# Retention in a fused two-layer kernel: who opens and who closes its first block

## The chip, the cores and the metric

The kernel runs on one core of a Trainium2 chip. The metric is the device time of one execution in microseconds (us), as the median of several executions. The engines are TensorE (PE in the profile, with PEld for its weight loads), VectorE (DVE), ScalarE (ACT), GpSimd (POOL) and SyncE (SP), which issues most of the DMAs.

## The reference, cut to what matters

Four sublayers run one after the other on `x` (8 batches of 256 rows, 512 columns) with the context `ctx_2048` of the same shape. The change lies in the first of them alone, retention with four heads of 128:

```
xn = layernorm(x)                                # 8 x 256 x 512
Q  = einsum('bshd,hde->bshe', xn,  Wh)
K  = einsum('bshd,hde->bshe', ctx, Wh)
V  = einsum('bshd,hde->bshe', ctx, Wh)
scores = einsum('bshe,bthe->bhst', Q, K) / sqrt(128)
masked = scores * Dn[None]                       # decay mask, never negative
A  = maximum(abs(masked.sum(axis=0)), 1.0)       # one A for all 8 batches
O  = einsum('hst,bthe->bshe', A, V)
Y  = (O - mean) / sqrt(var + 1e-3) * gamma + beta
x  = x + (relu(xn @ wg_w) * Y) @ wo_w
...                                              # bit FFN, mLSTM, mixture of experts
```

The scores are summed over the batches before the absolute value, so nothing of `O` can start until all eight batches have been scored.

## The kernel before, in words

`program` calls `retention`, then `bit_ffn`, `mlstm` and `experts`. `retention` has two blocks. A block is one program for each engine, and all engines meet at its end. Semaphores, set by hand, order the work inside it; each engine runs its own list in the written order.

**First block.** TensorE begins with a setup: it turns `wh` into `ring[0]` (L559, four transposes), clears the three score banks `acc` with products of zeros (L563), and forms `wht`ᵀ`wht` for each head (L566, the "gram"), so that `Q Kᵀ` needs one product with `gram` on the side of `xn` and none on the side of the context. The two results of the setup are copied out of PSUM by VectorE, as `wht` (L509) and `gram` (L511); only then does VectorE take the moments of the first 256 rows (L209 to L216), GpSimd raises the variance to the power -1/2 (L222) and VectorE writes `xn` (L482). TensorE waits for `gram` and for the load of `wg` before its first batch.

Then eight batches run. For one, TensorE turns `xn` and the context (L573, 16 transposes), multiplies `xt` by `gram` (L593, `q`), `ct` by `wh` (L600, `v`), `xt` by `wg` (L610, the gate) and adds the scores into `acc` (L616 into banks 0 and 1 for the first 128 context rows, L618 into bank 2 for the last 128). ScalarE copies `xt` and `qt` and writes the gate through a relu (L536, L540, L544). VectorE copies `ct` and `v` (L488, L505), normalises the next batch and centres the context (L493 to L495). SP stores `ct` and the centred context to `kt_d` and `vc_d`, and reloads `ctx_in` and `x`. Between batches, part of the ternary weights of the FFN is made (L358 on ScalarE, L371 to L383 on VectorE). The first four rounds of ScalarE are a loop, which holds an activation table load at its head.

When all eight batches are scored, VectorE makes `a_t` from `acc` with three instructions over all 1536 columns: times `decay` (L527), maximum of the value and its negative (L528), maximum with 1 (L529). The block ends there.

**Second block.** SP loads `wo`, `gn_gamma`, `gn_beta` and two more FFN weights. TensorE multiplies `a_t` by the values of batch 0 (`pv`, L709 and L712), waits while VectorE normalises the result, turns it (L724), does `pv` of the next batch, and multiplies by `wo` (L736).

Of the kernel before, what the change touches and what calls it, by code (L numbers as in the profile page):

```python
# [15 lines left out]
ALU = mybir.AluOpType  # L16
ACT = mybir.ActivationFunctionType
# [8 lines left out]
P = 128  # L26
B, S, D = 8, 256, 512
# [6 lines left out]
H0 = 4  # L34
# [302 lines left out]
def retention(nc, st, keep, sem, sbuf, psum, a, x, x_rows, ctx_rows, ident, powers, tern, w_mean, raw, vt, turned, kt_d, vc_d, upto):  # L337
    wt = sbuf(st, "gate_t", [P, KD, T])
    at = sbuf(st, "a_t", [P, H0 * (S + P)])
# [51 lines left out]
    with ExitStack() as sa:  # L391
        acc = psum(sa, "acc", [P, 3, 512])
        ring = [psum(sa, f"ring{i}", [P, 512]) for i in range(5)]
        decay = sbuf(sa, "decay", [P, H0 * (S + P)])
        wh = sbuf(sa, "wh", [P, H0, HD])
        wht = sbuf(sa, "wht", [P, H0, HD])
        gram = sbuf(sa, "gram", [P, H0, HD])
# [4 lines left out]
        ct = sbuf(sa, "ct", [P, KD, S])  # L402
        qt = sbuf(sa, "qt", [P, H0, S])
# [5 lines left out]
        ident_in, wh_in, wg_in, decay_in = (sem(n) for n in ("ident_in", "wh_in", "wg_in", "decay_in"))  # L409
        fill_done, dve_step = sem("fill_done"), sem("r_dve_step")  # L410
        setup_ps, setup_sb = sem("setup_ps"), sem("setup_sb")
        xn_ready, xt_ps, ct_ps, xt_sb, ct_sb = (sem(n) for n in ("xn_ready", "xt_ps", "ct_ps", "xt_sb", "ct_sb"))
        q_ps, v_ps, w_ps, q_sb, v_sb, w_sb = (sem(n) for n in ("q_ps", "v_ps", "w_ps", "q_sb", "v_sb", "w_sb"))
        scored, a_ready, kt_out, vc_ready = sem("scored"), sem("a_ready"), sem("kt_out"), sem("vc_ready")
        vc_out = [sem(f"vc_out{u}") for u in range(2)]
        block = sa.enter_context(nc.Block())
# [55 lines left out]
        @block.vector  # L472
        def _(dve):
            steps = Steps(dve, dve_step)

            def normalise(b, i, u):
                dve.wait_ge(x_in[u], 16 * i + 16)
                norm.stats(steps, [x[:, CB * b + c, :] if isinstance(b, int) else x[:, ds(CB * b + c, 1), :]
                                   for c in range(CB)], LN_EPS)
                dve.wait_ge(norm.rstd_ready, b + 1)  # L480
                for c in range(CB):
                    nc.vector.tensor_scalar(xn[:, c, :], x[:, ds(CB * b + c, 1), :], norm.mv[:, c, 0:1],  # L482
                                            norm.rstd[:, c:c + 1], ALU.subtract, ALU.mult).then_inc(xn_ready, 1)

            def copies(b, src_sem, counts, ring_at, dst, done):
                for c in range(CB):
                    dve.wait_ge(src_sem, 2 * b + c + 1)
                    nc.vector.tensor_copy(dst(c), ring[ring_at[c]][:].rearrange("p (k n) -> p k n", n=P)).then_inc(done, 1)  # L488

            def centre(u):  # L490

                heads = cx[:, u].rearrange("p c (h e) -> p c h e", e=DH)
                steps.then(nc.vector.tensor_reduce(vmean[:], heads, AX.X, ALU.add))  # L493
                steps.then(nc.vector.tensor_scalar(vmean[:], vmean[:], 1.0 / DH, None, ALU.mult))
                nc.vector.tensor_tensor(heads, heads, vmean[:].unsqueeze(3).to_broadcast([P, CB, NH, DH]),  # L495
                                        ALU.subtract).then_inc(vc_ready, 1)

            def batch(b, u, nxt):
                dve.wait_ge(kt_out, 16 * b + 16)
                copies(b, ct_ps, None, (1, 3), lambda c: ct[:, :, c * P:(c + 1) * P], ct_sb)  # L500
                if nxt is not None:
                    normalise(b + 1, *nxt)
                for c in range(CB):
                    dve.wait_ge(v_ps, 2 * b + c + 1)
                    nc.vector.tensor_copy(vt[:, ds(CB * b + c, 1), :], ring[1 + c][:]).then_inc(v_sb, 1)  # L505
                centre(u)

            dve.wait_ge(setup_ps, 1)
            nc.vector.tensor_copy(wht[:], ring[0][:].rearrange("p (h n) -> p h n", n=P)).then_inc(setup_sb, 1)  # L509
            dve.wait_ge(setup_ps, 2)  # L510
            nc.vector.tensor_copy(gram[:], ring[1][:].rearrange("p (h n) -> p h n", n=P)).then_inc(setup_sb, 1)  # L511
            normalise(0, 0, 0)
            dve.sem_inc(kt_out, 16)
            with steps.loop(0, B // 2 - 1, 12) as i:
                batch(2 * i, 0, (i, 1))
                batch(2 * i + 1, 1, (i + 1, 0))
            half = KF * D // 2
            dve.wait_ge(mean_ready, 1)
            ternary(steps, [(0, raw)], 0, half)
            batch(B - 2, 0, (B // 2 - 1, 1))  # L520
            ternary(steps, [(0, raw)], half, half)
            batch(B - 1, 1, None)

            dve.wait_ge(scored, B)
            dve.wait_ge(decay_in, 16)
            flat = acc[:].rearrange("p n d -> p (n d)")
            steps.then(nc.vector.tensor_tensor(at[:], flat, decay[:], ALU.mult))  # L527
            steps.then(nc.vector.scalar_tensor_tensor(at[:], at[:], -1.0, at[:], ALU.mult, ALU.max))  # L528
            nc.vector.tensor_scalar(at[:], at[:], 1.0, None, ALU.max).then_inc(a_ready, 1)  # L529

        @block.scalar
        def _(act):
            def batch(b):
                for c in range(CB):
                    act.wait_ge(xt_ps, 2 * b + c + 1)
                    nc.scalar.copy(xt[:, :, c * P:(c + 1) * P],  # L536
                                   ring[2 * c][:].rearrange("p (k n) -> p k n", n=P)).then_inc(xt_sb, 1)
                for c in range(CB):
                    act.wait_ge(q_ps, 2 * b + c + 1)
                    nc.scalar.copy(qt[:, :, c * P:(c + 1) * P],  # L540
                                   ring[(4, 0)[c]][:].rearrange("p (k n) -> p k n", n=P)).then_inc(q_sb, 1)
                for c in range(2):
                    act.wait_ge(w_ps, 2 * b + c + 1)
                    nc.scalar.activation(wt[:, 2 * c:2 * c + 2, ds(S * b, S)],  # L544
                                         ring[3 + c][:].rearrange("p (k n) -> p k n", n=S), ACT.Relu).then_inc(w_sb, 1)

            with act.Fori(0, B - 4) as b:
                batch(b)
            abs_sum(act, 0, raw)
            with act.Fori(B - 4, B) as b:  # L550
                batch(b)

        @block.tensor
        def _(pe):
# [3 lines left out]
            for h in range(H0):  # L558
                last = nc.tensor.transpose(ring[0][:, h * P:(h + 1) * P], wh[:, h, :], ident[:])  # L559
# [3 lines left out]
                nc.tensor.matmul(acc[:, n, :], zeros[:, 0:P], zeros[:], start=True, stop=False, skip_group_check=True)  # L563
            pe.wait_ge(setup_sb, 1)
            for h in range(H0):
                last = nc.tensor.matmul(ring[1][:, h * P:(h + 1) * P], wht[:, h, :], wht[:, h, :], start=True, stop=True)  # L566
            last.then_inc(setup_ps, 1)
            pe.wait_ge(setup_sb, 2)
            pe.wait_ge(wg_in, 16)

            def turn(dst, src, done):
                for k in range(KD):
# [3 lines left out]
            def batch(b, i, u, first=False):  # L576
                for c in range(CB):
# [7 lines left out]
                        pe.wait_ge(*((v_sb, 2 * b - 1), (w_sb, 2 * b - 1))[c])  # L585
                    turn(ring[2 * c + 1], cx[:, u, c, :], ct_ps)

                for c in range(CB):
                    pe.wait_ge(xt_sb, 2 * b + c + 1)
                    if c == 0 and not first:  # L590
                        pe.wait_ge(w_sb, 2 * b)
                    for h in range(H0):
                        last = nc.tensor.matmul(ring[(4, 0)[c]][:, h * P:(h + 1) * P], gram[:, h, :],  # L593
                                                xt[:, h, c * P:(c + 1) * P], start=True, stop=True)
                    last.then_inc(q_ps, 1)

                for c in range(CB):
# [3 lines left out]
                                                wh[:, h, :], start=True, stop=True)  # L601
                    last.then_inc(v_ps, 1)

                for n in range(2):
                    if n == 1:
                        pe.wait_ge(q_sb, 2 * b + 1)
                    for j in range(2):
                        m = 2 * n + j
                        for k in range(KD):
                            last = nc.tensor.matmul(ring[3 + n][:, j * S:(j + 1) * S], wg[:, k, m * P:(m + 1) * P],  # L610
                                                    xt[:, k, :], start=k == 0, stop=k == KD - 1)
                    last.then_inc(w_ps, 1)

                pe.wait_ge(q_sb, 2 * b + 2)
                for h in range(H0):
                    nc.tensor.matmul(acc[:, h // 2, (h % 2) * S:(h % 2 + 1) * S], ct[:, h, 0:P], qt[:, h, :],  # L616
                                     start=False, stop=False, skip_group_check=True)
                    last = nc.tensor.matmul(acc[:, 2, h * P:(h + 1) * P], ct[:, h, P:S], qt[:, h, P:S],  # L618
                                            start=False, stop=False, skip_group_check=True)
                last.then_inc(scored, 1)  # L620
# [2229 lines left out]
```

## Time and profile before

| | us |
|---|---|
| three executions | 1164.37, 1163.9, 1161.15 |
| median | 1163.9 |
| the profiled execution | 1158.16 |
| its span, from the first instruction to the last | 1156.4 |
| outside the span (1158.16 - 1156.4) | 1.76 |
| first block of retention, first to last instruction | 0 to 142.84 |

All times in the rows below are microseconds from the start of the span. TensorE is busy for 1075.6 of the 1156.4 us, VectorE for 839.1, ScalarE for 476.2 and GpSimd for 440.5. The granted clock is a share of TensorE's upper level of 2.4 GHz: 1.00 is that level, 0.50 is 1.2 GHz. Its mean over the span is 0.965.

### The profile page before, as it was taken

The numbers are of one execution on the slowest core, as the hardware profiler recorded it, in microseconds if no ns is written. First come the engines' busy times: TensorE is split into PE (matmuls) and PEld (weight loads), VectorE is DVE, ScalarE is ACT, GpSimd is POOL, SyncE is SP. The second block draws the span as 40 slices with busy tenths as digits, with TensorE's granted clock in tenths as the row PEclk, the third lists the DMA queues.
The fourth block names the chain that finished last, engine by engine and source line by source line (L and its number), as shares of the span: only waits on it lengthen the run. The fifth ranks groups of instructions, "written<-read, shape, count | busy, mean of one in ns | idle before, by whom it ended". The sixth has DMA issues, their size and how long they took to land. (4 is left out here: it accounts for less than half of the span.)

```text
span 1156.4 us, 21710 instructions
## 1 busy us (share of the span) xinstructions
PE 1075.6 (93%) x5911; PEld 814.0 (70%) x5912; DVE 839.1 (73%) x1578; ACT 476.2 (41%) x1009; POOL 440.5 (38%) x355
## 2 busy tenths in 40 slices
PE   6999889989998799999899987999999999999997
PEld 5989765634443458988887765777777777777773
DVE  4537545969998648778897994868688687766656
ACT  1342125336564269888521162333333333333320
POOL 0001011315442100667662001556665556666620
PEclk8999999999999898989889997999999999999998
DMA  7344162243233587755075313889899899887759
GB/s 275 128 146 154 56 244 41 46 83 69 56 68 60 156 266 261 254 191 183 1 266 201 65 56 126 238 191 246 190 259 264 202 261 252 196 200 189 138 120 367
DMA packets 148189, 195.49 MB, mean 169 GB/s; under 512 B 62985, under 2 KB 80777, under 8 KB 148144
## 3 DMA queue, kind: packets, MB, share of 16 engines
q1 hardware_dynamic: 130512, 156.61, 42.7%
q0 software_dynamic: 17632, 38.32, 16.7%
q8 instruction: 23, 0.38, 0.1%
q14 instruction: 22, 0.18, 0.0%
HBM read 136.56 MB, written 50.34 MB: 162 GB/s over the span
## 5 line engine op out<-in xcount | busy, mean ns | idle before, releaser
L2442 POOL DMA_INDIRECT y_d<-tail,x_ox x78 | 142.8, 1830 | 126.4 <-ACT tail L2669 105.8
L1718 POOL DMA_INDIRECT e_rows<-r_d,x_ix x80 | 101.6, 1270 | 115.5 <-issue 95.9
L2514 PE MATMUL x_h<-x_w_hi,x_t_hi 128*128 x320 | 127.8, 399 | 2.2 <-DVE x_t_lo L2683 2.2
L2515 PE MATMUL x_h<-x_w_lo,x_t_hi 128*128 x320 | 127.6, 399 | 0.0
L2516 PE MATMUL x_h<-x_w_hi,x_t_lo 128*128 x320 | 127.5, 399 | 0.0
L2683 DVE TENSOR_TENSOR x_w_lo<-w,x_w_hi (+1 forms) x64 | 112.5, 1759 | 9.8 <-ACT x_w_hi L2640 2.6
L2631 ACT ACTIVATE e_rows<-x_h 128x256 f32<-128x256 f32 x80 | 30.8, 385 | 183.7 <-PE x_h L2516 183.6
L222 POOL TENSOR_TENSOR ln_rstd<-ln_ve,powers 128x2 f32<-128x2 f32 (+1 forms) x40 | 34.5, 861 | 174.0 <-DVE ln_ve L216 174.0
L2683 DVE TENSOR_TENSOR x_t_lo<-x_xb,x_t_hi 128x512 fp32r<-128x512 f32 x80 | 55.2, 691 | 45.4 <-ACT x_t_hi L2626 43.7
L2533 PE MATMUL x_o<-x_w_hi,x_avt_hi 128*128 x160 | 74.0, 462 | 1.0 <-issue 0.7
L1595 DVE SCALAR_TENSOR_TENSOR raw<-h_qk,h_d 128x768 f32<-128x768 f32 x64 | 58.2, 952 | 22.1 <-ACT h_d L1362 10.1
L2514 PEld LDWEIGHTS x_h<-x_w_hi,x_t_hi 128*128 128x128 f32 x320 | 60.8, 190 | 17.5 <-issue 2.6
L2515 PEld LDWEIGHTS x_h<-x_w_lo,x_t_hi 128*128 128x128 f32 x320 | 60.8, 190 | 14.8
L2516 PEld LDWEIGHTS x_h<-x_w_hi,x_t_lo 128*128 128x128 f32 x320 | 60.7, 190 | 14.8
L1361 ACT ACTIVATE h_d<-h_negm,h_g 128x256 f32<-128x256 f32 x128 | 63.6, 497 | 6.2 <-DVE h_negm L1575 3.0
L736 PE MATMUL p_bank<-wo,z_t 128*128 128x512 f32 x128 | 58.3, 610 | 6.9 <-DVE z_t L799 6.9
L2730 DVE SCALAR_TENSOR_TENSOR e_rows<-e_rows,x_rw,x_h 128x256 f32<-128x256 f32 x80 | 38.2, 478 | 35.1 <-ACT e_rows L2631 34.4
L2534 PE MATMUL x_o<-x_w_lo,x_avt_hi 128*128 x160 | 63.3, 395 | 0.0
L610 PE MATMUL ring<-xt,wg 128*128 128x256 f32 x256 | 56.6, 379 | 0.0
L1488 PE MATMUL h_pv<-h_v,raw 128*128 128x99 f32 x256 | 55.3, 300 | 0.0
L2669 ACT COPY tail<-x_o 128x512 f32<-128x512 f32 x78 | 45.9, 589 | 18.6 <-PE x_o L2539 18.6
L1489 PE MATMUL h_pv<-h_v,raw 128*128 128x99 f32 x256 | 52.7, 290 | 0.0
(420 smaller groups left out, 2584.4 us busy)
## 6 DMA issues: line engine op xcount, KB each, us to landing
w<-in_L_ffn_w SPq DMA_DIRECT2D x32, 1024.0 KB, 9.5
w<-in_L_ffn_w SPq DMA_DIRECT2D x32, 512.0 KB, 8.5
h_negm<-negm_d SPq DMA_DIRECT2D x15, 1024.0 KB, 7.6
raw<-in_L_ffn_w SPq DMA_DIRECT2D x3, 2816.0 KB, 16.5
x_res<-in_x SPq DMA_DIRECT2D x8, 512.0 KB, 4.6
ctx_in<-in_ctx SPq DMA_DIRECT2D x8, 512.0 KB, 3.5
kt_d<-ct SPq DMA_DIRECT2D x8, 512.0 KB, 3.2
vc_d<-ctx_in SPq DMA_DIRECT2D x8, 512.0 KB, 2.6
```

What stands on the lines that cost most here:

```text
L610: last = nc.tensor.matmul(ring[3 + n][:, j * S:(j + 1) * S], wg[:, k, m * P:(m + 1) * P], xt[:, k, :], start=k == 0, stop=k == KD - 1)
L736: last = nc.tensor.matmul(p_bank[c][:], zt[:, c, k * P:(k + 1) * P], wo[:, k, :], start=k == 0, stop=k == KD - 1)
L1361: nc.scalar.activation(dm[:, k % 2, j, 0:2, :], nm[:, u, h, 0:2, :], ACT.Exp, bias=gst[:, u, 0, h:h + 1])
L1595: nc.vector.scalar_tensor_tensor(cm[:, k % 2, heads], qk[:, heads, 0:3 * P], float(DH) ** -0.5, dm[:, k % 2, heads].rearrange("p j c n -> ...
L1718: nc.gpsimd.indirect_dma_start(out=xg[q][s], out_offset=None, in_=r_d, in_offset=bass.IndirectOffsetOnAxis(ap=ix[q][:, s:s + 1], axis=0), ...
L2442: nc.gpsimd.indirect_dma_start(out=y_d[s], out_offset=bass.IndirectOffsetOnAxis(ap=ox[q][:, s:s + 1], axis=0), in_=eo[q][s][:], in_offset= ...
L2514: nc.tensor.matmul(hbank[s], hi[:, k, :], w13p[0][:, at, k, :], start=k == 0, stop=False)
L2515: nc.tensor.matmul(hbank[s], hi[:, k, :], w13p[1][:, at, k, :], start=False, stop=False)
L2516: last = nc.tensor.matmul(hbank[s], lo[:, k, :], w13p[0][:, at, k, :], start=False, stop=k == KD - 1)
L2533: nc.tensor.matmul(obank[s], hi[:, f, :], w2p[0][:, at, f, :], start=f == 0, stop=False)
L2534: nc.tensor.matmul(obank[s], hi[:, f, :], w2p[1][:, at, f, :], start=False, stop=False)
L2683: return nc.vector.tensor_tensor(dst, src, hi.bitcast(F32), ALU.subtract)
```

## The change

- VectorE no longer copies `wht` and `gram`. Its list begins with the moments of the first rows. ScalarE makes both copies, ahead of its loop over the batches, and the gram is formed in `ring[4]` instead of `ring[1]`.
- TensorE no longer waits for `gram` and `wg` ahead of its first transposes, but ahead of the first product that reads each.
- In every batch the four products L616 come before the four L618, and the semaphore `scored` counts each bank by itself.
- `a_t` is formed bank by bank. ScalarE writes the absolute value of a bank of `acc` to `a_t`; VectorE multiplies it by `decay` in place and takes the maximum with 1. The decay mask is never negative, so the absolute value may come first.

```diff
             def batch(b, u, nxt): ...
-            dve.wait_ge(setup_ps, 1)
-            nc.vector.tensor_copy(wht[:], ring[0][:].rearrange("p (h n) -> p h n", n=P)).then_inc(setup_sb, 1)
-            dve.wait_ge(setup_ps, 2)
-            nc.vector.tensor_copy(gram[:], ring[1][:].rearrange("p (h n) -> p h n", n=P)).then_inc(setup_sb, 1)
             normalise(0, 0, 0)
...
-            dve.wait_ge(scored, B)
             dve.wait_ge(decay_in, 16)
-            flat = acc[:].rearrange("p n d -> p (n d)")
-            steps.then(nc.vector.tensor_tensor(at[:], flat, decay[:], ALU.mult))
-            steps.then(nc.vector.scalar_tensor_tensor(at[:], at[:], -1.0, at[:], ALU.mult, ALU.max))
-            nc.vector.tensor_scalar(at[:], at[:], 1.0, None, ALU.max).then_inc(a_ready, 1)
+            def decayed(n):
+                dve.wait_ge(abs_scores, n + 1)
+                mine = slice(n * D, (n + 1) * D)
+                return nc.vector.tensor_tensor(at[:, mine], at[:, mine], decay[:, mine], ALU.mult)
+            def floored(n):
+                mine = at[:, n * D:(n + 1) * D]
+                nc.vector.tensor_scalar(mine, mine, 1.0, None, ALU.max).then_inc(a_ready, 1)
+            steps.then(decayed(0))
+            floored(0)
+            steps.did(decayed(1))
+            steps.then(decayed(2))
+            floored(1)
+            floored(2)
...
+            act.wait_ge(setup_ps, 1)
+            nc.scalar.copy(wht[:], ring[0][:].rearrange("p (h n) -> p h n", n=P)).then_inc(setup_sb, 1)
+            act.wait_ge(setup_ps, 2)
+            nc.scalar.copy(gram[:], ring[4][:].rearrange("p (h n) -> p h n", n=P)).then_inc(setup_sb, 1)
             with act.Fori(0, B - 4) as b:
...
+            for n in range(3):
+                act.wait_ge(scored, 3 * B - 2 + n)
+                nc.scalar.activation(at[:, n * D:(n + 1) * D], acc[:, n, :], ACT.Abs).then_inc(abs_scores, 1)
...
-                last = nc.tensor.matmul(ring[1][:, h * P:(h + 1) * P], wht[:, h, :], wht[:, h, :], start=True, stop=True)
+                last = nc.tensor.matmul(ring[4][:, h * P:(h + 1) * P], wht[:, h, :], wht[:, h, :], start=True, stop=True)
             last.then_inc(setup_ps, 1)
-            pe.wait_ge(setup_sb, 2)
-            pe.wait_ge(wg_in, 16)
```

TensorE's list at the very start, before: the first product of a batch (`ring<-ident,xn`) stands behind three waits, `setup_sb` among them.

```order
L559 MATMUL ring<-ident,wh 128x128 [waits fill_done,wh_in,ident_in]
L559 MATMUL ring<-ident,wh 128x128 x3
L563 MATMUL acc<-zeros 128x512 x3
L566 MATMUL ring<-wht 128x128 [waits setup_sb]
L566 MATMUL ring<-wht 128x128 x3
L573 MATMUL ring<-ident,xn 128x128 [waits xn_ready,wg_in,setup_sb]
L573 MATMUL ring<-ident,xn 128x128 x3
L573 MATMUL ring<-ident,ctx_in 128x128 [waits ctx_in0]
```

The same place now, up to the gate's first product (`ring<-xt,wg`):

```order
L574 MATMUL ring<-ident,wh 128x128 [waits fill_done,wh_in,ident_in]
L574 MATMUL ring<-ident,wh 128x128 x3
L578 MATMUL acc<-zeros 128x512 x3
L581 MATMUL ring<-wht 128x128 [waits setup_sb]
L581 MATMUL ring<-wht 128x128 x3
L586 MATMUL ring<-ident,xn 128x128 [waits xn_ready]
L586 MATMUL ring<-ident,xn 128x128 x3
...
L608 MATMUL ring<-xt,gram 128x128 [waits xt_sb,setup_sb]
...
L627 MATMUL ring<-xt,wg 128x256 [waits wg_in]
```

The wait for `gram` moved behind the 16 transposes, and the wait for `wg` behind the products `q` and `v` too.

VectorE's list at the end of the first block, before, from the last batch's copies of `v` on:

```order
L505 COPY v_rows<-ring 128x512 [waits v_ps] x2
L493 TENSOR_REDUCE v_mean<-ctx_in 128x32
L494 TENSOR_SCALAR v_mean<-v_mean 128x32 [waits r_dve_step]
L495 TENSOR_TENSOR ctx_in<-ctx_in,v_mean 128x1024 [waits r_dve_step]
L527 TENSOR_TENSOR a_t<-acc,decay 128x1536 [waits decay_in,scored]
L528 SCALAR_TENSOR_TENSOR a_t<-a_t 128x1536 [waits r_dve_step]
L529 TENSOR_SCALAR a_t<-a_t 128x1536 [waits r_dve_step]
```

The same place now; ahead of it, as the last instruction of its own list in this block, ScalarE has `L566 ACTIVATE a_t<-acc 128x512 [waits scored] x3`, a line number of the changed file.

```order
L506 COPY v_rows<-ring 128x512 [waits v_ps] x2
L494 TENSOR_REDUCE v_mean<-ctx_in 128x32
L495 TENSOR_SCALAR v_mean<-v_mean 128x32 [waits r_dve_step]
L496 TENSOR_TENSOR ctx_in<-ctx_in,v_mean 128x1024 [waits r_dve_step]
L526 TENSOR_TENSOR a_t<-a_t,decay 128x512 [waits abs_scores,decay_in]
L530 TENSOR_SCALAR a_t<-a_t 128x512 [waits r_dve_step]
L526 TENSOR_TENSOR a_t<-a_t,decay 128x512 [waits abs_scores] x2
L530 TENSOR_SCALAR a_t<-a_t 128x512 [waits r_dve_step]
L530 TENSOR_SCALAR a_t<-a_t 128x512
```

Three instructions over 1536 columns became three products and three maxima over 512 columns, and the absolute value went to ScalarE.

## Rows read from the trace of the kernel before

**Rows 1.** The page: TensorE over the whole span, then its granted clock in tenths.

```profile
PE 1075.6 (93%) x5911; PEld 814.0 (70%) x5912; DVE 839.1 (73%) x1578; ACT 476.2 (41%) x1009; POOL 440.5 (38%) x355
PEclk8999999999999898989889997999999999999998
```

**Rows 2.** Timeline, first 15 us: start, duration, engine, line, operation, count, [idle before <-releaser].

```profile
8.34 1.92 PE L566 MATMUL ring<-wht 128*128 128x128 f32 x8
10.29 0.69 DVE L511 COPY gram<-ring 128x512 f32<-128x512 f32 x1 [2.30 <-PE ring L566]
10.90 1.28 DVE L209 BATCH_NORM_STATS2 ln_st<-x_res 128x6 f32<-128x512 f32 x2
14.34 1.09 PE L573 MATMUL ring<-ident,xn 128*128 128x128 f32 x4 [4.08 <-DVE xn L482]
```

**Rows 3.** DMA issues at 0.7, 2.2, 2.75, 18 us; last number is us to landing.

```profile
x_res<-in_x SPq DMA_DIRECT2D x1, 512.0 KB, 3.5
...
ctx_in<-in_ctx SPq DMA_DIRECT2D x1, 512.0 KB, 6.2
...
wg<-in_L_xattn_wg_w SPq DMA_DIRECT2D x1, 1024.0 KB, 8.4
...
kt_d<-ct SPq DMA_DIRECT2D x1, 512.0 KB, 5.0
```

**Rows 4.** Windows: stretch, length, busy of PE, PEld, DVE, ACT, POOL, clock, DMA, GB/s.

```profile
10.30:13.60 3.30, 0.00 (x0) 0.00 (x0) 2.35 (x7) 0.00 (x0) 0.72 (x1) 1.00 1.05 389
14.30:17.80 3.50, 3.46 (x17) 3.49 (x18) 1.04 (x2) 1.17 (x2) 0.00 (x0) 0.50 1.05 388
17.80:20.40 2.60, 2.60 (x14) 2.60 (x14) 2.31 (x7) 0.59 (x1) 0.00 (x0) 0.50 1.04 387
```

**Rows 5.** Timeline of TensorE: batch 0's `v` and gate, then batch 7's transposes and `v`.

```profile
20.82 1.95 PE L600 MATMUL ring<-wh,ct 128*128 128x128 f32 x16
22.61 7.07 PE L610 MATMUL ring<-xt,wg 128*128 128x256 f32 x32
...
123.25 0.60 PE L573 MATMUL ring<-ident,xn 128*128 128x128 f32 x4
...
126.78 1.95 PE L600 MATMUL ring<-wh,ct 128*128 128x128 f32 x16
```

**Rows 6.** Waits from 30 to 138 us, TensorE's only one: total, times, longest.

```profile
PE ring L593 <- ACT xt L536: 1.8, 1, 1.8
```

**Rows 7.** Timeline at the end of the first block and the start of the second.

```profile
135.76 0.60 ACT L544 ACTIVATE gate_t<-ring 128x512 f32 x1 [2.86 <-PE ring L610]
137.87 0.38 PE L618 MATMUL acc<-qt,ct 128*128 128x128 f32 x2
138.29 1.76 DVE L527 TENSOR_TENSOR a_t<-acc,decay 128x1536 f32<-128x1536 f32 x1 [6.23 <-PE acc L618]
141.88 0.96 DVE L529 TENSOR_SCALAR a_t<-a_t 128x1536 f32<-128x1536 f32 x1
143.17 0.66 PE L709 MATMUL o_bank<-v_rows,a_t 128*128 128x128 f32 x2 [4.92 <-PEq L391]
```

**Rows 8.** Groups of instructions, 0 to 160 us: busy, mean ns of one, idle before.

```profile
L377 DVE TENSOR_SCALAR raw<-raw 128x2816 f32<-128x2816 f32 x2 | 3.3, 1628 | 0.1
L799 DVE TENSOR_TENSOR z_t<-z_t,gate_t 128x512 f32<-128x512 f32 x2 | 1.4, 691 | 2.4 <-ACT z_t L756 2.4
```

**Rows 9.** Windows of the second block; columns as in rows 4.

```profile
143.40:146.70 3.30, 3.30 (x17) 3.30 (x17) 0.00 (x0) 0.00 (x0) 0.00 (x0) 0.50 0.62 189
153.60:156.90 3.30, 3.30 (x18) 3.30 (x17) 1.38 (x2) 2.35 (x7) 0.00 (x0) 0.50 1.06 400
183.30:185.80 2.50, 0.00 (x0) 0.00 (x0) 2.36 (x9) 1.67 (x2) 0.55 (x1) 1.00 0.51 101
185.80:193.00 7.20, 7.18 (x18) 3.31 (x19) 4.38 (x11) 7.20 (x3) 1.50 (x4) 1.00 0.00 0
```

**Rows 10.** Issue of `gn_beta` at 144.1 us, with its time to landing.

```profile
gn_beta<-in_L_xattn_gn_beta SPq DMA_DIRECT2D x1, 2.0 KB, 5.1
```

**Rows 11.** Timeline of ScalarE between batches 0 and 1.

```profile
30.42 1.28 ACT L536 ACT_TABLE_LOAD   x1
32.77 0.59 ACT L536 COPY xt<-ring 128x512 f32<-128x512 f32 x1 [1.06 <-PE ring L573]
```

**Rows 12.** Windows: first and last of ten later stretches at the lower clock.

```profile
242.30:245.70 3.40, 3.40 (x5) 1.34 (x5) 1.86 (x2) 1.02 (x2) 0.00 (x0) 0.50 0.09 19
...
710.00:720.10 10.10, 6.05 (x18) 4.82 (x19) 5.96 (x6) 4.33 (x7) 0.00 (x0) 0.50 0.39 141
```

More of the change, by code:

```diff
@@ L413, in retention @@
         q_ps, v_ps, w_ps, q_sb, v_sb, w_sb = (sem(n) for n in ("q_ps", "v_ps", "w_ps", "q_sb", "v_sb", "w_sb"))
+        abs_scores = sem("abs_scores")
         scored, a_ready, kt_out, vc_ready = sem("scored"), sem("a_ready"), sem("kt_out"), sem("vc_ready")
@@ L586, in batch @@
                     turn(ring[2 * c + 1], cx[:, u, c, :], ct_ps)
+                if first:
+                    pe.wait_ge(setup_sb, 2)
                 for c in range(CB):
@@ L602, in batch @@
                     last.then_inc(v_ps, 1)
+                if first:
+                    pe.wait_ge(wg_in, 16)
                 for n in range(2):
@@ L615, in batch @@
                 for h in range(H0):
-                    nc.tensor.matmul(acc[:, h // 2, (h % 2) * S:(h % 2 + 1) * S], ct[:, h, 0:P], qt[:, h, :],
-                                     start=False, stop=False, skip_group_check=True)
+                    last = nc.tensor.matmul(acc[:, h // 2, (h % 2) * S:(h % 2 + 1) * S], ct[:, h, 0:P], qt[:, h, :],
+                                            start=False, stop=False, skip_group_check=True)
+                    if h % 2:
+                        last.then_inc(scored, 1)
+                for h in range(H0):
                     last = nc.tensor.matmul(acc[:, 2, h * P:(h + 1) * P], ct[:, h, P:S], qt[:, h, P:S],
```

## The prediction

> **What bounds the kernel.** I read the page first, then the timeline of the first 30 us, then the timeline and the waits around the block's end at 138 us, and last the granted clock of the same stretches. TensorE is busy for 93% of the span [rows 1], and inside the eight batches it waits once, for 1.8 us, between 30 and 138 us [rows 6]. So the first block is a chain of TensorE work with a hole at each end, and what shortens a hole moves everything after it. The reader is to see the two holes. TensorE ends the gram at 8.34 + 1.92 = 10.26 and starts its first transposes at 14.34, after 4.08 us in which VectorE copies `gram` and only then opens the moments [rows 2]. It ends the scores at 137.87 + 0.38 = 138.25 and starts on `a_t` at 143.17, 4.92 us later, while VectorE runs three long instructions [rows 7]. A third thing is seen in the clock: the work that follows each hole runs at the lower level, 1.2 GHz (0.50), from 14.3 to 20.4 and from 143.4 to 146.7 [rows 4, 9].
>
> **Head, the hole.** From VectorE's first moment to TensorE's first transpose the chain takes 14.34 - 10.90 = 3.44 us [rows 2]. The rows that it needs are issued at the start of the program and take 3.5 us to land [rows 3]; the issue lies between 0.7 and 1.2 us, so they are there by 4.7 at the latest. `xn` is then ready at about 4.7 + 3.4 = 8.1, ahead of 10.26. TensorE's setup itself stays as long: ScalarE's copy of `wht` takes about as long as its 0.59 us copy of `xt` [rows 11], against 0.69 for a VectorE copy of 512 columns [rows 2], and it is hidden by the clearing products. The transposes can start at 10.26: **4.08 us are gone**. What is late next? The context is issued by 2.7 and takes 6.2, so it lands by 8.9; `wg` is issued by 3.2 and takes 8.4, so by 11.6, and its first reader now comes after the transposes, `q` and `v`, not before 15 [rows 3]. The gram copy on ScalarE (0.6 us, to about 10.9) stands ahead of the first copy of `xt` in ScalarE's queue; that copy can't start before TensorE has turned four blocks (0.6 to 1.1 us, by the level of the clock [rows 2, 5], from 10.26), so at most 0.2 us is added there, and TensorE has the other transposes to do meanwhile. Nothing else is queued behind the two copies. The store of `ct` now comes some 6 us earlier, under the load of the FFN weights; before it was issued at 18.9 and took 5.0 us [rows 3]. VectorE waits for it only ahead of batch 1's `ct`, more than 8 us after the issue in either kernel; I count nothing.
>
> **Head, the clock.** The trace grants 1.00 from 10.3 to 13.6, where TensorE has nothing to do, just after the matmuls of the setup. It grants 0.50 from 14.3 on, through the transposes and until 20.4, when 2.6 us of matmuls have run [rows 4]. From the first transpose to the start of `v` takes 20.82 - 14.34 = 6.48 us in batch 0 and 126.78 - 123.25 = 3.53 us in batch 7 at the upper level [rows 5]. So that stretch costs 2.95 us for the level alone. With the hole closed the batch falls into the stretch that is granted 1.00, directly behind 3 us of setup matmuls, and in the steady batches a block of 16 transposes between matmuls keeps 1.00. I take the whole **2.95 us**. The bounds are 0 (the clock stays low for as much work as before) and 2.95.
>
> **Table loads.** ScalarE's loop carried a table load of 1.28 us in each of its rounds; now one stands ahead of the loop. ScalarE was idle for 1.06 us behind the load, waiting for TensorE [rows 11]. That wait is the cover, and the gain is nothing. The one load left has 5 us before `wht` is asked for.
>
> **Inside the batches.** The scores are the same eight products in another order, with two more increments. No engine waits for them before the last batch. Nothing, within 0.1 us a batch.
>
> **Tail, the hole.** The last product still ends at 138.25, in this trace's times. Bank 0 is complete about 1.8 us ahead, bank 1 about 0.9 us ahead. ScalarE ends the gate's relu at 136.36 [rows 7] and is free for bank 0. The absolute value of a bank has no row of its own; the relu of 512 columns from PSUM takes 0.60 [rows 7], and that is what I take (0.59 for a copy, rows 11, is the other end). Bank 2: 138.3 + 0.60 = 138.9. VectorE's product of 512 columns in SBUF takes 0.69 [rows 8]; banks 0 and 1 are done by 138.95, bank 2 runs to 139.65. The maximum with 1 is 0.96 for 1536 columns and 1.63 for 2816 [rows 7, 8], so 0.67 / 1280 a column, and 0.96 - 1024 x 0.00052 = 0.42 for 512; by a share of a third it would be 0.32. Two of them end at 139.7 + 0.42 + 0.35 = 140.45. Before, the chain ended at 141.88 + 0.96 = 142.84. **The gain is 2.4 us** (2.2 to 2.6 with the bounds of the two unseen durations), and the meeting of the engines behind it, 143.17 - 142.84 = 0.33, stays. What the three whole instructions cost and the pieces don't is hidden under TensorE's last products.
>
> The trace has 0.69 for a product of 512 columns where a third of 1.76 would be 0.59 [rows 7, 8], so each piece pays a fixed part. The Trainium skill, "VectorE: DVE Perf Modes", section "Rules for kernel authors", says that chained VectorE operations should be cut in number, which speaks against six in place of three. Taken alone it would make the tail three fixed parts longer, three times about 0.15 us by these rows, and the sum smaller by that 0.45 us; the rows show why it does not decide, since four of the six lie beside other work.
>
> **Tail, the clock.** `pv` of batch 0 runs at 0.50 from 143.4 to 146.7 [rows 9]. At the upper level these 3.3 us of work are 1.65. The hole ahead of it shrinks from 4.92 to 2.5 us. The nearest row is a hole of 2.5 us from 183.3 to 185.8, after which the clock stays at 1.00 [rows 9]. Against it: after the next hole of 3.7 us, which stays, the clock falls again at 153.6. The bounds are 0 and 1.65; which executions keep the clock will differ, and I count the middle, **0.8 us**. Nothing else holds this back: `gn_beta`, issued by 144.4, lands by 149.5, and moves with the block [rows 10]; TensorE's next transposes came 9.1 us after the block's start, and would come at 7.5, when it has landed at 6.3.
>
> **Sum.** 4.08 + 2.95 + 2.4 + 0.8 = 10.2 us. Against the profiled execution's own 1158.16 that is 1147.9. That execution was 5.7 us below the median of the runs shown, 1163.9; all of its holes are before the same semaphores, so I take the difference from the median: **1153.7 us**.
>
> **Rivals.**
> - *The clock stays low through the head (20%).* From 14.3 to 17.8 TensorE did transposes only, at 0.50, and the level rose only after matmuls [rows 4]. If the 16 transposes behind the gram drop or hold it, batch 0 runs as slowly as before and only the hole is gained: 4.08 + 2.4 + 0 to 1.65 = 6.5 to 8.1, about 1156.6. For it: 3.5 us of transposes did not raise the clock. Against it: in batch 7 the same transposes ran at full pace [rows 5]. The Trainium skill, "TensorE: Matmul & The Clock Gate", section "Part 4: PE-mode transpose", says that transposes don't count as activity in the way matmuls do; by that rule this rival would hold. Batch 0's rows agree with it, and batch 7's do not refute it, since matmuls stand close on both sides there.
> - *The clock stays up in both places (25% of the forecast's 70%).* 4.08 + 2.95 + 2.4 + 1.65 = 11.1, so 1152.8.
> - *The head does not open early (5%).* If VectorE or GpSimd starts late, because `xn` hangs on something that the trace of before did not show (its first moments at 10.90 were behind a copy, so no earlier start was ever seen), only the tail is left: 2.4 to 4.1, so 1160 to 1161.5, within what a measurement tells from no change. The same holds if the change does not do what it says.
> - *Slower (3%).* Behind 160 us there are ten stretches at 0.50, 60 us together, the first of 3.4 us and the last of 10.1 [rows 12], each after an idle spell of TensorE in the later layers. The change moves the later program against the clock's grants by 10 us. A stretch of 3.4 us costs at most 1.7. To end over 0.3% slower, it must lose 10.2 + 3.5 = 13.7 us, eight more such stretches, which gives 1168. The executions of before, which differ in just this way, spread over 6.2 us from 1158.16 to 1164.37, so half of that price is not seen.
>
> **How the numbers follow.** The forecast (one or the other tail clock, full head) has 70%, with 1151 to 1155.5 as its own span; the low-clock head 20%; the late head 5%; slower 3%; a gain above 13 us 2%. The executions differ by some 3 us about their median, and 0.3% of 1163.9 is 3.5 us, about what a measurement of this kernel can tell from no change. The range runs from 1163.9 - 11.1 - 3 = 1149.8 to 1163.9 - 6.5 + 2.5 = 1159.9. Faster by over 0.3% (below 1160.4) 0.90, within it 0.07, slower 0.03.
>
> **What would show it right or wrong.** In the profile after: the first moments near 4.5 us; the first `xn` transposes with no idle before them, at 10.3; the granted clock at 1.00 until past 20; the gate products of batch 0 starting near 15.6 and not 22.6. At the end of the block: ScalarE's third absolute value 0.6 us long, the last maximum 2.2 us behind TensorE's last score, and `pv` 2.5 us behind it, at about 0.1 us a product if the clock held, and not at 0.2 (17 products in 3.3 us, rows 9). Between the two, the batches at an unchanged pitch. It is wrong if TensorE waits for `gram`, `ct` or `wg` in batch 0, if the batches lose what the head gains, or if the later layers give it back.

## The result

| | before | changed |
|---|---|---|
| median of four executions, us | 1163.05 | 1150.22 |
| lowest and highest | 1161.15 to 1164.37 | 1146.71 to 1151.06 |
| profiled execution | 1158.16 | 1151.06 |
| its span | 1156.4 | 1149.2 |

The ratio is 0.9898, with a 95% interval from 0.9871 to 0.9925: 12 us less, 8.7 to 15.0. Timed again, six executions of the changed kernel had a median of 1149.42 against 1160.57 for seventeen of before, a ratio of 0.9898 once more (0.9876 to 0.9920), 11.8 us less. What was expected of this second timing was 9.4 to 11.1 us less, with a rival of 12 us or more that would mean something beyond the two ends of the block; its interval, from 9.3 to 14.4 us, holds both. The forecast was 1153.7 in a range from 1149.8 to 1159.9, a gain of 10.2 us. The measured median lies near the low end of that range, and 0.8 us below the 1151 to 1155.5 that the forecast gave as its own span.

### The profile page after: what moved, and what is told of

Read it like the earlier page. It is cut to its first block and busy times, and to the rows that moved or that the text cites. A ratio compares the mean times of both kernels' runs of the same rounds, so it can differ in the third digit from the quotient of the medians.

```text
span 1149.2 us, 21701 instructions
## 1 busy us (share of the span) xinstructions
PE 1072.1 (93%) x5899; PEld 813.8 (71%) x5912; DVE 836.3 (73%) x1579; ACT 475.3 (41%) x1011; POOL 444.5 (39%) x355
## 5 line engine op out<-in xcount | busy, mean ns | idle before, releaser
L2534 PEld LDWEIGHTS x_h<-x_w_hi,x_t_hi 128*128 128x128 f32 x320 | 60.9, 190 | 17.5 <-issue 2.6
```

What stands on the lines that cost most here:

```text
L2534: nc.tensor.matmul(hbank[s], hi[:, k, :], w13p[0][:, at, k, :], start=k == 0, stop=False)
```

## The profile after

TensorE's share of the span is the same 93% as in [rows 1]; what it waits for has changed. The timeline of TensorE at the start, to be held against [rows 2] (line numbers are those of the changed file: L586 was L573, L581 was L566):

```profile
8.70 1.76 PE L581 MATMUL ring<-wht 128*128 128x128 f32 x8
10.30 0.60 PE L586 MATMUL ring<-ident,xn 128*128 128x128 f32 x4
```

No idle time stands at the first transposes, they start at 10.30 and not at 14.34, and four of them take 0.60 us and not 1.09. What feeds them, from the same timeline:

```profile
4.28 1.28 DVE L209 BATCH_NORM_STATS2 ln_st<-x_res 128x6 f32<-128x512 f32 x2 [4.13 <-DMA x_res<-in_x]
7.03 1.00 DVE L483 TENSOR_SCALAR xn<-x_res,ln_mv,ln_rstd 128x512 f32<-128x512 f32 x2 [0.92 <-POOL ln_rstd L222]
10.50 0.59 ACT L558 COPY gram<-ring 128x512 f32<-128x512 f32 x1 [2.24 <-PE ring L581]
13.83 1.95 PE L615 MATMUL ring<-wh,ct 128*128 128x128 f32 x16
15.62 7.07 PE L627 MATMUL ring<-xt,wg 128*128 128x256 f32 x32
```

VectorE waits for the first rows, and `xn` is there two microseconds before TensorE wants it. The gate's products of batch 0 start at 15.62, against 22.61 in [rows 5]: 7.0 us ahead. In the batches that follow TensorE waits once, for the same 1.8 us as in [rows 6].

The end of the block, against [rows 7] (L638 was L618, L729 was L709):

```profile
129.55 0.60 ACT L566 ACTIVATE a_t<-acc 128x512 f32<-128x512 f32 x1 [0.18 <-PE acc L633]
130.21 1.05 PE L638 MATMUL acc<-qt,ct 128*128 128x128 f32 x8
130.25 0.69 DVE L526 TENSOR_TENSOR a_t<-a_t,decay 128x512 f32<-128x512 f32 x1 [5.18 <-ACT a_t L566]
131.30 0.60 ACT L566 ACTIVATE a_t<-acc 128x512 f32<-128x512 f32 x1 [0.29 <-PE acc L638]
131.32 1.31 DVE L526 TENSOR_TENSOR a_t<-a_t,decay 128x512 f32<-128x512 f32 x2
132.66 0.76 DVE L530 TENSOR_SCALAR a_t<-a_t 128x512 f32<-128x512 f32 x2
133.75 0.46 PE L729 MATMUL o_bank<-v_rows,a_t 128*128 128x128 f32 x2 [2.49 <-PEq L391]
```

The last score ends at 131.26 and VectorE's last maximum at 133.42, 2.16 us later. TensorE's hole is 2.49 us and was 4.92. `pv` starts 9.42 us ahead of before.

The granted clock, from the windows of the changed kernel (stretch, length, busy of PE, PEld, DVE, ACT, POOL, clock, DMA, GB/s), against [rows 4, 9]:

```profile
10.30:13.90 3.60, 3.60 (x35) 3.60 (x34) 2.35 (x4) 2.25 (x4) 0.00 (x0) 1.00 1.03 380
13.90:20.40 6.50, 6.50 (x40) 5.93 (x40) 5.44 (x12) 1.18 (x2) 0.71 (x1) 1.00 1.05 390
133.80:137.50 3.70, 3.70 (x32) 3.57 (x32) 0.00 (x0) 0.00 (x0) 0.05 (x2) 1.00 0.61 217
141.30:146.40 5.10, 5.10 (x24) 5.10 (x25) 1.93 (x3) 2.90 (x8) 0.00 (x0) 0.50 1.05 394
```

Batch 0 runs at the upper level all through, and so does `pv` of batch 0. The low stretch behind the next hole, 3.4 us long in the trace of before, is 6.8 us long here, from 139.9 to 146.7. That length is not the change's doing: in a second profile of the kernel before, the same stretch is 6.8 us long too, from 151.7 to 158.5.

**Where the time went, stage by stage.** The table gives, for each profiled execution, the start of the last product with `wo` (the end of the second block, within a microsecond) and what is left from there to the end of the span. The rows below the first four are the experiments of the next section.

| execution | last product with `wo` | from there to the end |
|---|---|---|
| before | 250.3 | 906.1 |
| before, again | 251.6 | 906.7 |
| changed | 240.0 | 909.2 |
| changed, again | 239.2 | 908.7 |
| head alone | 242.9 | 908.2 |
| tail alone | 246.7 | 911.9 |
| tail alone, again | 247.7 | 910.0 |
| before, head filled | 248.1 | 912.3 |
| before, tail filled | 249.5 | 908.2 |
| changed, both holes filled | 237.9 | 910.8 |
| changed, second hole filled | 238.8 | 909.1 |
| changed, gram first | 239.4 | 908.2 |
| changed, more transposes | 246.4 | 905.3 |
| changed, more products | 246.6 | 909.8 |

The first column holds the change: 250.3 and 251.6 before, 240.0 and 239.2 after, 11.4 us between the means. The second column belongs to layers that no edit touches, and it runs from 905.3 to 912.3 in no order that the edits explain: the two profiles of the changed kernel lie about 2.5 us above the two of before, but the two kernels that are before with a hole filled, which share nothing with the change, lie 1.8 and 5.9 us above them. Single executions therefore differ by several microseconds, and the two profiled executions of the head of this section, 7.1 us apart, understate the change.

## Experiments

Each was timed against the kernel before on the same chip. As a scale, the kernel before was timed against itself:

> The kernel before, timed against itself. Both theories: a ratio of 1 within 0.25%, which says how far the other ratios can be trusted. Its profile should show the hole of 4.1 us at the head with the clock at 0.50 behind it, the hole of 4.9 us at the tail, and the last product with wo near 250; from there to the end of the span 905 to 913 us, as in the other executions, whatever was done in the first block.

Measured: ratio 0.9996 (0.9973 to 1.0020), medians 1161.09 and 1161.89. So differences under about 2.5 us are not shown by times alone, and the profiles have to tell them.

**The head alone.** The copies of `wht` and `gram` on ScalarE, VectorE opening with the moments, the two waits of TensorE moved; the scores and `a_t` as before.

```diff
-            dve.wait_ge(setup_ps, 1)
-            nc.vector.tensor_copy(wht[:], ...).then_inc(setup_sb, 1)
-            dve.wait_ge(setup_ps, 2)
-            nc.vector.tensor_copy(gram[:], ...).then_inc(setup_sb, 1)
...
+            act.wait_ge(setup_ps, 1)
+            nc.scalar.copy(wht[:], ...).then_inc(setup_sb, 1)
+            act.wait_ge(setup_ps, 2)
+            nc.scalar.copy(gram[:], ...).then_inc(setup_sb, 1)
```

> Only the head of the change: VectorE opens with the moments, ScalarE copies wht and gram, TensorE's waits for gram and wg moved; scores and a_t as before. Theory: 4.1 for the hole and 2.95 for the clock, so 7.0 us less than before, pv starting near 136.2, and the clock at 0.50 in pv of batch 0 as before. Rival that the clock is no part of it: 4.1 us.

Measured: ratio 0.9941 (0.9917 to 0.9964), 6.8 us less (4.2 to 9.6). Its `pv` starts at 135.77, 7.4 us ahead of the first profile of before and 6.4 us ahead of the second, behind the old hole and at the old pace:

```profile
135.77 0.47 PE L711 MATMUL o_bank<-v_rows,a_t 128*128 128x128 f32 x2 [4.92 <-PEq L391]
135.70:139.10 3.40, 3.33 (x17) 3.36 (x18) 0.00 (x0) 0.00 (x0) 0.13 (x2) 0.56 0.58 191
```

The first line is from its timeline, the second from its windows. The 4.1 us of the rival are just outside the interval, and the profile rules them out: from the first transpose to `v` it takes 3.54 us, where before takes 6.48.

**The tail alone**, timed twice: the scores by bank, ScalarE's absolute value and VectorE's pieces; the head as before.

```diff
+            for n in range(3):
+                act.wait_ge(scored, 3 * B - 2 + n)
+                nc.scalar.activation(at[:, n * D:(n + 1) * D], acc[:, n, :], ACT.Abs).then_inc(abs_scores, 1)
```

> Only the tail of the change: scores counted by bank, ScalarE's absolute value, VectorE bank by bank; the head as before. Theory: 2.4 us for the hole, 0 to 1.65 for the clock in pv of batch 0, so 2.4 to 4.1 less than before. Batch 0 has the hole of 4.1 us and the low clock as before. Rival that the two ends don't add up (the tail's gain hangs on the head): less than 2 us.

Measured: ratio 0.9944 (0.9921 to 0.9966), 6.5 us less (3.9 to 9.2). That was more than the theory allows for, and I timed it once more.

> The tail of the change alone once more. Theory: 2.4 to 4.1 us less than before; the 6.5 us of its first timing, with an interval from 3.9 to 9.2, were the spread of the later layers. Rival (the tail is worth more than its hole and one low stretch): again 5 us or more.

Measured: ratio 0.9973 (0.9948 to 0.9998), 3.1 us less (0.2 to 6.0), and in the table its second block ends 4.3 and, in the second profile, 3.3 us ahead of the mean of before. The rival's 5 us or more lie inside the interval, but the table speaks against them: what the first timing had on top was the spread. The second profile also holds something that the changed kernel's does not: here the hole of 2.5 us did cost the clock. The products L727 and L730 of its `pv` go from 0.39 us a pair to 0.63:

```profile
139.61 0.46 PE L727 MATMUL o_bank<-v_rows,a_t 128*128 128x128 f32 x2 [2.49 <-PEq L391]
139.91 0.39 PE L730 MATMUL o_bank<-v_rows,ones 128*128 128x128 f32 x2
140.13 0.39 PE L727 MATMUL o_bank<-v_rows,a_t 128*128 128x128 f32 x2
140.35 0.56 PE L730 MATMUL o_bank<-v_rows,ones 128*128 128x128 f32 x2
140.71 0.63 PE L727 MATMUL o_bank<-v_rows,a_t 128*128 128x128 f32 x2
```

**The head's hole kept, but filled.** The kernel before, with 15 products of zeros by zeros between the gram and the wait for it. They add nothing to the cleared bank.

```diff
             last.then_inc(setup_ps, 1)
+            for _ in range(15):
+                nc.tensor.matmul(acc[:, 0, :], zeros[:, 0:P], zeros[:], start=False, stop=False, skip_group_check=True)
             pe.wait_ge(setup_sb, 2)
```

> The kernel before, with 15 products of zeros by zeros (added onto the cleared score bank, which they leave as it is) in TensorE's hole between the gram and the first transposes. The hole stays as long, about 4.1 us, but TensorE is at work in it. Clock theory: the granted clock is 1.00 from 10 to 24 us, the first transpose stays at about 14.3, v of batch 0 starts 3.5 us behind it and not 6.5, and the kernel is 2.95 us faster. Rival (the clock of batch 0 is set by the transposes and not by the hole): 0.50 from 14 to 20 as before, no gain.

Measured: ratio 0.9980 (0.9959 to 1.0002), 2.3 us less (from 4.8 less to 0.2 more). The times alone would not show it; the profile does. Its timeline and its windows:

```profile
9.58 4.26 PE L569 MATMUL acc<-zeros 128*128 128x512 bf16 x15
13.87 0.63 PE L575 MATMUL ring<-ident,xn 128*128 128x128 f32 x4
17.43 1.84 PE L602 MATMUL ring<-wh,ct 128*128 128x128 f32 x15
14.30:17.80 3.50, 3.50 (x34) 3.50 (x33) 2.62 (x5) 1.93 (x4) 0.00 (x0) 1.00 1.04 387
```

From the first transpose to `v` are 17.43 - 13.87 = 3.56 us, where before had 6.48 [rows 5], at a clock of 1.00 where before had 0.50 [rows 4]. The hole is as long as it was (from 9.79 to 13.87). So of the head's 7 us, 2.9 are the clock, and they come from TensorE having been at work just before, not from anything in batch 0. The filling did more than keep a level: its 15 products take 4.26 us, 0.28 each, where the same product takes 0.22 in a profile further down (24 in 5.34 us). The first of them still ran at the lower pace, and the level came up while they ran.

**The tail's hole kept, but filled.** The kernel before, with 20 products of zeros behind the last batch.

```diff
                 batch(2 * i + 1, i, 1)
+            for _ in range(20):
+                nc.tensor.matmul(ring[0][:], zeros[:, 0:P], zeros[:], start=True, stop=True)
```

> The kernel before, with 20 products of zeros in TensorE's hole of 4.9 us ahead of pv; the hole stays as long. Clock theory: pv of batch 0 runs at 1.00 and ends 1.65 us sooner behind its start, so 1.65 us less than before. Rival (the gain of 6.5 us that the tail alone showed, against 2.4 to 4.1 expected, is the clock and is worth more than one low stretch): 3 us or more less than before.

Measured: ratio 0.9979 (0.9961 to 0.9997), 2.4 us less (0.3 to 4.5). `pv` of batch 0, in its windows, against the first line of [rows 9]:

```profile
142.80:146.40 3.60, 3.58 (x32) 3.60 (x32) 0.00 (x0) 0.00 (x0) 0.11 (x2) 1.00 0.66 184
```

Thirty-two products where before had 17 in 3.3 us. The rival's 3 us or more lie inside the interval, but the table has 1.5 us, and with the second timing of the tail nothing is left to explain.

**The changed kernel, its holes filled.** In one kernel 9 products of zeros in the hole of 2.5 us and 14 of ones by ones in the hole of 3.7 us behind `pv`; in the other the second set alone.

```diff
                 batch(2 * i + 1, i, 1)
+            for _ in range(9):
+                nc.tensor.matmul(ring[0][:], zeros[:, 0:P], zeros[:], start=True, stop=True)
...
             pv(0)
+            for _ in range(14):
+                nc.tensor.matmul(p_bank[0][:, 0:P], ones[:], ones[:], start=True, stop=True)
             pe.wait_ge(wo_in, 48)
```

> The changed kernel with 9 products of zeros (into a bank nobody reads any more) in TensorE's hole of 2.5 us at the end of the first block and 14 small products of ones by ones in its hole of 3.7 us behind pv of batch 0; both sets fit into their holes. Clock theory: nothing starts later, the low stretch from 139.6 to 146.4 of the changed kernel is gone, its 5.1 us of work take half, so 2.5 us less than the changed kernel, 12 to 14 us less than before. Rival (the low stretch there does not come from the hole, or only moves on): as the changed kernel.

> As after_filled_both, with only the hole of 3.7 us behind pv of batch 0 filled. If the hole of 2.5 us ahead of pv never costs the clock, this gains the same 2.5 us over the changed kernel; if it sometimes does, this gains less than after_filled_both by up to 1.65 us.

Measured: ratios 0.9895 (0.9876 to 0.9913) and 0.9885 (0.9864 to 0.9906), medians 1149.64 and 1147.34. The windows of the kernel with both, for the second hole and for what follows it:

```profile
137.60:141.50 3.90, 3.36 (x31) 3.17 (x29) 2.69 (x8) 0.00 (x0) 0.69 (x1) 1.00 0.89 277
141.50:146.20 4.70, 4.66 (x40) 4.45 (x41) 2.00 (x3) 2.90 (x8) 0.00 (x0) 1.00 1.05 395
```

The low stretch is gone, 40 products run where the changed kernel had 24, and the first product with `wo` comes 12.2 us behind `pv`'s start and not 14.6. The second block ends 1.7 us ahead of the mean of the changed kernel. In the whole time this can't be told from the changed kernel. In the kernel with the second hole filled alone a low stretch turned up from 173.5 to 176.8 us, where neither profile of the changed kernel has one, so in that execution a part of it may have moved on. Neither is shown to be faster than the change itself.

The kernel with both holes filled shows one thing more. Its head is that of the changed kernel, closed, and yet batch 0 begins at the lower pace:

```profile
9.82 1.06 PE L586 MATMUL ring<-ident,xn 128*128 128x128 f32 x4
10.67 0.93 PE L586 MATMUL ring<-ident,ctx_in 128*128 128x128 f32 x4
11.44 0.60 PE L586 MATMUL ring<-ident,xn 128*128 128x128 f32 x4
```

From the first transpose to `v` it takes 14.10 - 9.82 = 4.28 us, 0.75 more than the changed kernel. So a closed head does not always save the whole of the clock's price.

**The wait for gram back ahead of the transposes**, in the changed kernel.

```diff
             last.then_inc(setup_ps, 1)
+            pe.wait_ge(setup_sb, 2)
...
-                if first:
-                    pe.wait_ge(setup_sb, 2)
```

> The changed kernel, with TensorE's wait for gram put back ahead of its first transposes. Theory: TensorE stands from 10.3 until ScalarE has copied gram, about 11.1, so 0.8 us more than the changed kernel, with the clock at 1.00 all through batch 0. Rival (most of the head's gain comes from the moved wait): 4 us or more.

Measured: ratio 0.9904 (0.9878 to 0.9929), 11.1 us less than before. The timeline has the price of the wait, 0.68 us, with the transposes at full pace behind it:

```profile
10.35 0.66 PE L587 MATMUL ring<-ident,xn 128*128 128x128 f32 x4 [0.68 <-ACT gram L558]
10.84 0.60 PE L587 MATMUL ring<-ident,ctx_in 128*128 128x128 f32 x4
```

So the head's hole was closed by VectorE opening with the moments; moving the wait is worth the last 0.7 us of it. What moving the wait for `wg` is worth was not tried. In the changed kernel that load is issued at 2.8 to 3.3 and takes 8.2 us, so it lands at 11.0 to 11.5, behind the first transposes at 10.30: by these rows up to about 1 us may hang on it, an estimate.

**Do transposes hold the clock?** Two variants of the changed kernel with more work ahead of batch 0: 48 transposes of rows that are turned anyway, or 24 products of zeros.

```diff
+            pe.wait_ge(xn_ready, 1)
+            for _ in range(12):
+                for k in range(KD):
+                    nc.tensor.transpose(ring[2][:, k * P:(k + 1) * P], xn[:, 0, k * P:(k + 1) * P], ident[:])
             batch(0, 0, 0, first=True)
```

> The changed kernel with 48 more transposes of the same rows ahead of batch 0, some 5.3 us at the upper level. If transposes hold the clock as matmuls do, it stays at 1.00 and batch 0 starts 5.3 us later. If they don't, the clock falls to 0.50 in or right behind them, the last of them are twice as far apart, and part of batch 0 runs at half pace: 7 to 9 us later than the changed kernel.

> The partner of after_more_turns: 24 products of zeros by zeros in place of the 48 transposes, some 5.2 us at the upper level. Both theories: the clock stays at 1.00 and batch 0 starts 5.2 us later than in the changed kernel.

Measured: 1153.45 and 1158.19, one execution each, so nothing rests on these times. The timeline and the windows of the kernel with more transposes, and last the 24 products of its partner:

```profile
9.55 5.58 PE L645 MATMUL ring<-ident,xn 128*128 128x128 f32 x48
14.96 0.60 PE L586 MATMUL ring<-ident,xn 128*128 128x128 f32 x4
16.71 1.95 PE L608 MATMUL ring<-xt,gram 128*128 128x128 f32 x16
9.60:15.00 5.40, 5.40 (x50) 5.40 (x49) 0.00 (x0) 0.59 (x1) 0.00 (x0) 1.00 1.05 395
15.00:16.70 1.70, 1.70 (x18) 1.70 (x16) 0.66 (x1) 0.81 (x2) 0.00 (x0) 1.00 1.05 389
10.13 5.34 PE L644 MATMUL ring<-zeros 128*128 128x512 bf16 x24
```

For 7.1 us, from 9.55 to 16.71, TensorE did nothing but transposes, and the last of them still run at the upper pace, 0.60 us for four, as they do behind the products. That is one execution, of float32 transposes that began about when the level came up.

Whether transposes can also bring a low clock up is seen in the second profile of the tail alone, whose head is that of before. Its timeline, then its windows:

```profile
14.79 1.09 PE L588 MATMUL ring<-ident,xn 128*128 128x128 f32 x4 [4.08 <-DVE xn L483]
17.38 0.69 PE L588 MATMUL ring<-ident,ctx_in 128*128 128x128 f32 x4
17.90 1.95 PE L608 MATMUL ring<-xt,gram 128*128 128x128 f32 x16
14.80:17.50 2.70, 2.70 (x13) 2.70 (x14) 0.99 (x2) 0.59 (x1) 0.00 (x0) 0.50 1.05 388
17.60:17.90 0.30, 0.30 (x4) 0.30 (x4) 0.00 (x0) 0.28 (x1) 0.00 (x0) 1.00 1.08 403
```

The clock fell to 0.50 at 14.1, inside the hole. From 14.79 on TensorE did only transposes, and at 17.5, before the first product with `gram` at 17.90, it was back at 1.00. So they can, in this one execution; in the other four with the open hole it came back among the products of `q`.

## Why the prediction was right

**The head's hole, 4.08 us: right.** The first transposes moved from 14.34 to 10.30, and the cover named for every later input held: `xn` by 8.0, `gram` copied by 11.1, nothing waited for in batch 0. **The head's clock, 2.95 us: the mechanism right and its cause shown, the size taken at its largest.** From the first transpose to `v` the changed kernel takes 13.83 - 10.30 = 3.53 us, against 6.48. The filled hole gives the same 2.9 with the hole kept. Of the profiled executions, all five with the open hole had a low stretch in batch 0 (one of them by its pace alone, see the last section). It took them 6.48, 5.66, 6.34, 4.90 and 6.37 us from the first transpose to `v`, so the price was between 1.4 and 2.95 us, 2.4 in the mean. Of the nine with the hole closed or filled, eight took 3.5 to 3.6 us, and one took 4.28 (the changed kernel with both later holes filled). The whole of the head was 7.0 us in the first pair of profiles, as forecast, and 6.8 in the second (21.64 - 14.80 at the gate's first product).

**The rival of the transposes fell.** It had 20%, and rested on transposes that ran at 0.50 without raising the clock. The extra transposes show that they hold a level that is already there, and the second profile of the tail alone that they can run a low one up. The Trainium skill, "TensorE: Matmul & The Clock Gate", section "Part 4: PE-mode transpose", says that transposes don't count as activity in the way matmuls do; here the run of 64, still at the upper pace at its end, and the rise at 17.5 in the midst of transposes speak against it for this case, and the measurement decides.

**The tail's hole, 2.4 us: right.** 4.92 - 2.49 = 2.43, with the pieces as costed: 597 ns for the absolute value, 690 for a product and 424 for a maximum of 512 columns, in the grouped rows of the changed kernel:

```profile
L526 DVE TENSOR_TENSOR a_t<-a_t,decay 128x512 f32<-128x512 f32 x3 | 2.0, 690 | 5.2 <-ACT a_t L566 5.2
L566 ACT ACTIVATE a_t<-acc 128x512 f32<-128x512 f32 x3 | 1.8, 597 | 0.7 <-PE acc L633 0.4 <-PE acc L638 0.3
L530 DVE TENSOR_SCALAR a_t<-a_t 128x512 f32<-128x512 f32 x3 | 1.2, 424 | 0.1
```

One point of it was only touched on, where banks 0 and 1 are done by 138.95 and the last absolute value by 138.9: VectorE works without a pause from 130.25 to 133.42, so the last bank does not set the end alone. Bank 0's absolute value, at 129.55, starts a chain on VectorE of six pieces that is as long.

**The tail's clock, 0.8 us as the middle of 0 and 1.65: the right mechanism, but the upper bound was too low.** In both profiled executions of the changed kernel the whole price was saved: from `pv`'s start to VectorE's first look at its result are 3.85 us, where the first profile of before had 5.47. The bound of 1.65 came from that one trace, in which the clock falls at 143.3, just behind `pv`'s start. In the second profile of before it falls at 141.5, inside the hole, and stays low until 148.3:

```profile
142.30:148.00 5.70, 5.70 (x27) 5.70 (x28) 0.00 (x0) 0.00 (x0) 0.00 (x0) 0.50 0.75 207
```

There the same stretch takes 148.93 - 142.20 = 6.73 us. Over the four executions with the hole of 4.9 us the price was 1.6, 2.9, 1.6 and 2.2 us. Of the eight profiled executions with a hole of 2.5 us, five kept the clock in `pv` of batch 0 and three lost it (the second of the tail alone and the two with more work ahead); all four with the hole of 4.9 us lost it, and neither of the two with it filled did.

**What the sum left out.** By VectorE's first look at `pv` the changed kernel was 148.64 - 137.60 = 11.04 us ahead in the profiled pair, and by the first product with `wo` 158.64 - 148.34 = 10.30: the clock fell once more behind the next hole, for 6.8 us against 3.4 in this pair. I had named that hole and left its cost unchanged, and the second profile of before, with 6.8 us there too, does not contradict that. Over the two blocks the gain is 11.4 us in the means of two executions each, and 10.2 was forecast. The terms, in the same means and up to VectorE's first look at `pv` (11.6 us): the head's hole, with the setup ahead of it, 4.4 where the sum had 4.08; the head's clock 2.5 where it had 2.95; the tail's hole 2.4 as forecast; the tail's clock 2.25 where it had 0.8. The tail's clock is the term that was mis-sized, and part of it is hidden by the head's clock, which was counted too high.

**The step down to the median** was right in sign. I took the sum off the median of before and not off the profiled execution, 5.7 us lower. The table gives half of a reason: that execution's later layers took 906.1 us, against 908.9 in the mean of the fourteen, 2.8 us of the 5.7. The measured gain of 12 us, with its interval from 8.7 to 15.0, holds both 10.2 and 11.4, and the times alone don't say whether the whole is more than the two blocks show. The slower rival had the same mechanism, later stretches at the lower clock, and it is real, as spread: the second column of the table spans 7.0 us. It didn't move with the change.

## What to carry to other kernels

A hole in TensorE's work costs its own length and then again, because the work behind it can run at half pace; here the second price was 1.4 to 2.9 us for a hole of 4.1 (five executions) and 1.6 to 2.9 for one of 4.9 (four). One trace is not enough to size it: in the two profiles of the kernel before, the clock fell at different places of the same hole and stayed low for 3.4 us in one and 6.8 us in the other. Look at who makes the first operand of a stage, and let that engine open with it; copies that the same engine does on the side go to one that is idle. Where a chain of elementwise steps stands behind the last product, cut it by bank, so that little more than the last bank's share is left when TensorE stops (2.2 us here, where the whole chain took 4.6).

## What the runs showed that I had not expected

- A hole of 2.5 us is on the edge: ahead of `pv` it cost the clock in three of eight executions. The two profiles of the tail alone are of one and the same program, and one kept the clock there while the other lost it. The hole that the prediction took as its nearest row, at 183.3 in the trace of before, went both ways too: in the kernel before with its tail filled it is 2.6 us long, and the clock falls at 183.8, just behind it.
- Products of zeros are enough to have the upper level behind a hole of 4 to 5 us, without a delay to what follows; at the tail they kept it, at the head it came up while they ran.
- The clock column can't be read ahead of the first change that a trace holds. In the second profile of before, windows and timeline say for one stretch:

```profile
14.20:17.70 3.50, 3.50 (x17) 3.50 (x18) 0.99 (x2) 1.17 (x2) 0.00 (x0) 1.00 1.04 387
14.19 1.09 PE L573 MATMUL ring<-ident,xn 128*128 128x128 f32 x4 [4.08 <-DVE xn L482]
```

The column says 1.00, but four transposes in 1.09 us and 17 in 3.5 us are the pace that [rows 2, 4] have at 0.50; at the upper level they are 0.60 and 34. The pace of known instructions decides. The setup is such a stretch in every profile here: its column reads 1.00, but the eight products of the gram take 1.63 to 1.92 us, where sixteen of that shape take 1.95 in the batches. So the setup ran at the lower level for nearly all of its length, and in the changed kernel the level came up only about when the first transposes began.
